# First stage: normalisation moved to the scalar engine, low parts to Pool, three sets of part buffers

## What is computed

```python
x = x + L0_xattn(_layernorm(x), ctx, ctx, Wq, Wk, Wv, Wo)      # softmax attention, 16 heads of 16
x = x + L0_ffn(_layernorm(x), ...)                              # ternary weights, 8-bit levels, width 1024
x = x + L1_xattn(_layernorm(x), ctx, ctx, ifgate_w, ...)        # gated linear attention, 8 heads of 32
x = x + L1_ffn(_layernorm(x), weight, gate_w, lora_U, lora_V)   # dense plus gated low-rank

def _layernorm(x, axis=-1, eps=1e-05):
    m = jnp.mean(x, axis=axis, keepdims=True)
    v = jnp.var(x, axis=axis, keepdims=True)
    return (x - m) / jnp.sqrt(v + eps)
```

## Time and profile before

| | |
|---|---|
| Median of three runs | 512.41 us (507.75, 512.41, 512.77) |
| The profiled execution | 512.96 us |
| Its span in the trace | 511.2 us |
| PE busy | 379.1 us (74%) |
| DVE busy | 322.7 us (63%) |
| ACT busy | 258.3 us (51%) |
| Pool busy | 188.3 us (37%) |
| Mean granted clock of TensorE | 0.868 of full speed |

### The profile page before, as it was taken

One profiled execution on the slowest core, in us unless ns is written; L12 is line 12 of the kernel. 1 busy time (PEld: TensorE's weight loads), 2 busy tenths in 40 slices (PEclk: granted clock), 3 DMA queues, 4 the chain that ended last, 5 costly groups with the idle time before them and its releaser, 6 DMA issues.

```text
span 511.2 us, 8639 instructions
## 1 busy us (share of the span) xinstructions
PE 379.1 (74%) x2897; PEld 260.6 (51%) x2897; DVE 322.7 (63%) x1040; ACT 258.3 (51%) x486; POOL 188.3 (37%) x220
## 2 busy tenths in 40 slices
PE   3986597898878893447776667663778999999955
PEld 3774354665656561123533434442666676776722
DVE  3885433366445575377889879743357877877752
ACT  2644233643534552567887987854243443543521
POOL 1119300000000001787898898850014334333330
PEclk9998867879999996565888998987599999999975
DMA  6699987645465400000000000000021221221100
GB/s 205 201 291 270 298 274 184 131 80 135 107 123 111 78 2 1 1 2 0 1 1 1 1 1 1 1 1 1 0 42 42 43 63 48 48 62 48 26 21 21
DMA packets 53675, 37.91 MB, mean 74 GB/s; under 512 B 21632, under 2 KB 49664, under 8 KB 53504
## 3 DMA queue, kind: packets, MB, share of 16 engines
q1 hardware_dynamic: 53120, 37.31, 29.3%
q10 hardware_dynamic: 512, 0.07, 0.2%
HBM read 28.90 MB, written 8.39 MB: 73 GB/s over the span
## 4 chain that ended last, share of the span: by engine, by line
PE 28%; DVE 19%; issue 19%; POOL 11%; DMA 11%; ACT 8%; SPq 3%; ACTq 0%; POOLq 0%; DVEq 0%
POOL rr L472 5%; DMA QT<-negmT 5%; PE PS L1108 4%; PE PS L1206 4%; DMA qst<-negmT 4%; DVE h L637 3%; PE PS L1097 3%; PE PS L1088 2%; DVE negm L577 2%; DMA scr_k<-kpart 2%; ACT pT L913 2%; SPq L311 2%; PE PS L1166 2%; POOL smd L464 2%; PE PS L1125 1%
## 5 line engine op out<-in xcount | busy, mean ns | idle before, releaser
L913 ACT ACTIVATE pT<-PS 128x512 f32<-128x512 f32 x64 | 36.5, 596 | 68.4 <-PE PS L1088 67.9
L577 DVE TENSOR_REDUCE negm<-PS 128x4 bf16<-128x512 f32 x64 | 42.5, 686 | 41.9 <-PE PS L1097 41.6
L447 POOL TENSOR_TENSOR sm<-sm,mhalf 128x1 f32<-128x1 f32 x16 | 9.2, 574 | 142.2 <-DVE sm L678 142.2
L435 POOL TENSOR_TENSOR kst<-kst,rows 128x1024 f32<-128x1024 f32 x16 | 38.3, 2393 | 3.3 <-ACT kst L983 3.3
L437 POOL TENSOR_TENSOR kst<-kst,rows 128x1024 f32<-128x1024 f32 x16 | 38.2, 2386 | 1.3
L472 POOL TENSOR_TENSOR rr<-ms,mhalf 128x8 f32<-128x8 f32 x16 | 26.4, 1649 | 31.1 <-DVE ms L860 31.1
L1280 PEld LDWEIGHTS PS<-QT,kBD 128*128 128x128 f32 x256 | 34.6, 196 | 0.9
L1280 PE MATMUL PS<-QT,kBD 128*128 128x128 f32 x256 | 34.6, 279 | 0.0
L1108 PE MATMUL PS<-pT,vx 128*32 128x128 f32 x512 | 29.9, 309 | 3.6 <-ACT pT L913 3.5
L628 DVE SCALAR_TENSOR_TENSOR pT<-PS,sm,rows 128x1024 f32<-128x1024 f32 x16 | 20.5, 1284 | 17.4 <-PE PS L1206 17.2
L1189 PE MATMUL PS<-w2q,h2T 128*128 128x256 bf16 x128 | 18.4, 292 | 17.5 <-ACT h2T L955 17.5
(11 more groups left out here) (222 smaller groups left out, 1045.4 us busy)
## 6 DMA issues: line engine op xcount, KB each, us to landing
scr_q<-qpart SPq DMA_DIRECT2D x8, 384.0 KB, 4.8
scr_k<-kpart SPq DMA_DIRECT2D x8, 384.0 KB, 5.5
rows<-in_rows SPq DMA_DIRECT2D x1, 2056.0 KB, 9.5
X<-in_x SPq DMA_DIRECT2D x8, 256.0 KB, 4.5
CTXT<-in_ctxT SPq DMA_DIRECT2D x8, 256.0 KB, 4.8
cTb<-in_ctxT SPq DMA_DIRECT2D x16, 128.0 KB, 3.4
kBD<-in_ctxT SPq DMA_DIRECT2D x64, 32.0 KB, 1.9
vx<-in_ctx SPq DMA_DIRECT2D x16, 128.0 KB, 2.6
```

Of the source, the lines that this page charges most:

```text
L435: gp.tensor_tensor(n2[p.slot], n2[p.slot], ln2g, ALU.mult).then_inc(b_g2, 1)
L577: v.tensor_reduce(negm[:, 4 * hg:4 * hg + 4], PS[:, 2 + hg % 2, :].rearrange("p (h k) -> p h k", h=4), AX_X, ALU.max, negate=True).then_in ...
L913: s.activation(pT[:, hg, :], PS[:, hg % 2, :], ACT.Exp, scale=float(DH0) ** -0.5).then_inc(a_e, 1)
```

## The change

ACT takes over the normalisation as `Identity` with a scale and a bias from memory (1/sigma and minus mean over sigma), at the start of its turn. DVE makes minus the mean (`nm`), Pool the product `mr` after its power. Pool takes over the two subtractions that make the low parts, ahead of its power in each turn, and has one turn stage more. A third set of `qpart` and `kpart` lies in `kBD`, which stage C uses later. Pool waits for all its low parts before it begins its list of constants.

```diff
...
+        mr = [sb(f"mr{i}", [128, GP]) for i in range(2)]; nm = [sb(f"nm{i}", [128, GP]) for i in range(2)]
...
-        qpart = [sb(f"qpart{i}", [128, PARTS, GP, KC * S], BF16) for i in range(2)]
-        kpart = [sb(f"kpart{i}", [128, PARTS, GP, KC * S], BF16) for i in range(2)]
+        kBD = [sb(f"kBD{i}", [128, 4, KC, S]) for i in range(2)]
+        third = [kBD[i][:].rearrange("p j c t -> p (j c t)").bitcast(BF16)[:, 0:PARTS * GP * KC * S]
+                 .rearrange("p (n j x) -> p n j x", n=PARTS, j=GP) for i in range(2)]
+        qpart = [sb(f"qpart{i}", [128, PARTS, GP, KC * S], BF16)[:] for i in range(2)] + [third[0]]
+        kpart = [sb(f"kpart{i}", [128, PARTS, GP, KC * S], BF16)[:] for i in range(2)] + [third[1]]
...
-        p_stored = [sem(f"p_parts_stored{i}") for i in range(2)]
+        p_stored = [sem(f"p_parts_stored{i}") for i in range(3)]; p_pw = sem("p_power_ready")
...
                 for buf, scr in ((qpart, scr_q), (kpart, scr_k)):
                     sp.dma_start(scr[g].rearrange("n j p x -> p (n j) x"),
-                                 buf[g % 2][:].rearrange("p n j x -> p (n j) x")).then_inc(p_stored[g % 2], 16)
+                                 buf[g % 3].rearrange("p n j x -> p (n j) x")).then_inc(p_stored[g % 3], 16)
...
-                if isinstance(at.b, int):
-                    g = at.b // GP
-                    sp.wait_ge(p_stored[g % 2], (g // 2 + 1) * STORED)
+                g = at.b // GP
+                sp.wait_ge(p_stored[g % 3], (g // 3 + 1) * STORED)
...
-            def turn_p(f, _ln, _b):
+            def turn_p(f, _ln, _b, c):
+                if c:
+                    for n, buf, ready in ((0, kpart, p_low), (1, qpart, p_parts)):
+                        flat = [buf[c.b % 3][:, i].rearrange("p j (c t) -> p j c t", c=KC) for i in range(PARTS)]
+                        pool.wait_ge(p_mid, c.b * 2 + n + 1)
+                        gp.tensor_tensor(flat[2], rest[n][:].rearrange("p (j c t) -> p j c t", j=GP, c=KC), flat[1],
+                                         ALU.subtract).then_inc(ready, 1)
                 if f:
                     pool.wait_ge(p_ve, f.b + 1)
                     done(pool, p_ln, f, -1)
-                    gp.tensor_tensor(rs[f.slot % 2][:], ve[f.slot % 2][:], mhalf[:, 0:GP], ALU.pow).then_inc(p_rs, 1)
-
-            pipeline(pool, NG, 4, 3, turn_p)
+                    gp.tensor_tensor(rs[f.slot % 2][:], ve[f.slot % 2][:], mhalf[:, 0:GP], ALU.pow).then_inc(p_pw, 1)
+                    pool.wait_ge(p_pw, f.b + 1)
+                    gp.tensor_tensor(mr[f.slot % 2][:], nm[f.slot % 2][:], rs[f.slot % 2][:], ALU.mult).then_inc(p_rs, 1)
+
+            pipeline(pool, NG, 4, 4, turn_p)
             pool.wait_ge(p_rs, NG)
+            pool.wait_ge(p_low, NG)
+            pool.wait_ge(p_parts, NG)
...
             for i in range(2):
                 step(gp.memset(vx2[i][:, :, DH1:64], 1.0))
+                pool.wait_ge(p_stored[2], STORED * (NG // 3))
                 step(gp.memset(kBD[i][:], 0.0))
...
-            def turn_p(f, a, b, c):
-                def parts(at, n):
...
-                def part_low(n):
-                    _product, flat, r4 = parts(c, n)
-                    dve.wait_ge(p_mid, c.b * 2 + n + 1)
-                    return v.tensor_tensor(flat[2], r4, flat[1], ALU.subtract)
...
                     dve.wait_ge(p_hi, b.b * 2 + n + 1)
-                    v.tensor_tensor(r4, product, flat[0], ALU.subtract).then_inc(p_rest, 1)
-
-                if a:
-                    dve.wait_ge(p_rs, a.b + 1)
-                    done(dve, p_tr, a, -1)
-                    for i in range(GP):
-                        last = v.tensor_scalar(lnb[a.slot % 2][:, i, :], X[:, a.b * GP + i, :], mv[a.slot % 2][:, i, 0:1],
-                                               rs[a.slot % 2][:, i:i + 1], ALU.subtract, ALU.mult)
-                    last.then_inc(p_ln, 1)
-                if c:
-                    part_low(0).then_inc(p_low, 1)
-                    part_low(1).then_inc(p_parts, 1)
+                    v.tensor_tensor(rest[n][:].rearrange("p (j c t) -> p j c t", j=GP, c=KC),
+                                    PS[:, bank + b.slot % 2, :].rearrange("p (c j t) -> p j c t", c=KC, j=GP),
+                                    buf[b.b % 3][:, 0].rearrange("p j (c t) -> p j c t", c=KC),
+                                    ALU.subtract).then_inc(p_rest, 1)
+
                 if f:
                     dve.wait_ge(p_x[f.slot], 32 * (f.used + 1))
                     c1.start(f)
@@ -521,11 +511,14 @@
                     f_bn = c1.mark(v.bn_stats(st[f.slot % 2][:, 6:12], X[:, f.b * GP + 1, :]))
...
+                    done(dve, p_ln, f, -1)
                     v.bn_aggr(mv[f.slot % 2][:, 0, :], st[f.slot % 2][:, 0:6])
...
                     done(dve, p_rs, f, -1)
+                    v.tensor_scalar(nm[f.slot % 2][:], mv[f.slot % 2][:, :, 0], -1.0, None, ALU.mult)
                     v.tensor_scalar(ve[f.slot % 2][:], mv[f.slot % 2][:, :, 1], EPS, None, ALU.add).then_inc(p_ve, 1)
                     c1.end()
...
-            pipeline(dve, NG, 4, 4, turn_p)
+            pipeline(dve, NG, 4, 3, turn_p)
...
-                    flat = [buf[b.slot % 2][:, i].rearrange("p j (c t) -> p j c t", c=KC) for i in range(2)]
+                    flat = [buf[b.b % 3][:, i].rearrange("p j (c t) -> p j c t", c=KC) for i in range(2)]
...
-                if b:
-
-                    if not (isinstance(b.b, int) and b.b < 2):
-                        act.wait_ge(p_stored[b.slot % 2], (b.used * 2 + b.slot // 2) * STORED)
+                if f:
+                    act.wait_ge(p_rs, f.b + 1)
+                    done(act, p_tr, f, -1)
+                    for i in range(GP):
+                        last = s.activation(lnb[f.slot % 2][:, i, :], X[:, f.b * GP + i, :], ACT.Identity,
+                                            scale=rs[f.slot % 2][:, i:i + 1], bias=mr[f.slot % 2][:, i:i + 1])
+                    last.then_inc(p_ln, 1)
+                if b:
+
+                    if b.b >= 3:
+                        act.wait_ge(p_stored[b.b % 3], b.b // 3 * STORED)
                     mid_k = high(0, p_k, 4, kpart)
...
```

More of the change, by code:

```diff
@@ L231, in build @@
         g_a = sem("g_a_parts_chain"); g_m = sem("g_max_parts_chain")
-        kBD = [sb(f"kBD{i}", [128, 4, KC, S]) for i in range(2)]
         vx2 = [sb(f"vx2{i}", [128, H1, 64]) for i in range(2)]
@@ L330, in turn_a @@
                 if f and not (isinstance(f.b, int) and f.b < 4):
-                    if not isinstance(f.b, int) and f.slot == 0:
-                        for i in range(2):
-                            sp.wait_ge(p_stored[i], NG // 2 * STORED)
                     load_stacks(f)
@@ L486, in _, with turn_p, part_rest @@
             c1 = Chain(dve, p_st, 2)
-            def turn_p(f, a, b, c):
-                def parts(at, n):
+            def turn_p(f, _a, b):
+                def part_rest(n):
                     bank, buf = ((4, kpart), (2, qpart))[n]
-                    return (PS[:, bank + at.slot % 2, :].rearrange("p (c j t) -> p j c t", c=KC, j=GP),
-                            [buf[at.slot % 2][:, i].rearrange("p j (c t) -> p j c t", c=KC) for i in range(PARTS)],
-                            rest[n][:].rearrange("p (j c t) -> p j c t", j=GP, c=KC))
-                def part_low(n):
-                    _product, flat, r4 = parts(c, n)
-                    dve.wait_ge(p_mid, c.b * 2 + n + 1)
-                    return v.tensor_tensor(flat[2], r4, flat[1], ALU.subtract)
-                def part_rest(n):
-                    product, flat, r4 = parts(b, n)
-                    dve.wait_ge(p_hi, b.b * 2 + n + 1)
-                    v.tensor_tensor(r4, product, flat[0], ALU.subtract).then_inc(p_rest, 1)
-                if a:
-                    dve.wait_ge(p_rs, a.b + 1)
-                    done(dve, p_tr, a, -1)
-                    for i in range(GP):
-                        last = v.tensor_scalar(lnb[a.slot % 2][:, i, :], X[:, a.b * GP + i, :], mv[a.slot % 2][:, i, 0:1],
-                                               rs[a.slot % 2][:, i:i + 1], ALU.subtract, ALU.mult)
-                    last.then_inc(p_ln, 1)
-                if c:
-                    part_low(0).then_inc(p_low, 1)
-                    part_low(1).then_inc(p_parts, 1)
+                    dve.wait_ge(p_hi, b.b * 2 + n + 1)
+                    v.tensor_tensor(rest[n][:].rearrange("p (j c t) -> p j c t", j=GP, c=KC),
+                                    PS[:, bank + b.slot % 2, :].rearrange("p (c j t) -> p j c t", c=KC, j=GP),
+                                    buf[b.b % 3][:, 0].rearrange("p j (c t) -> p j c t", c=KC),
+                                    ALU.subtract).then_inc(p_rest, 1)
                 if f:
```

## The result

| | before | changed |
|---|---|---|
| Median, runs of the first comparison | 511.53 us (4 runs, 507.75 to 512.77) | 520.66 us (4 runs, 516.82 to 521.80) |
| Median, a later comparison | 511.72 us (17 runs) | 519.89 us (6 runs) |
| Profiled execution, span | 512.96, 511.2 us | 520.18, 518.4 us |
| PE, DVE, ACT, Pool busy | 379.1, 322.7, 258.3, 188.3 us | 373.1, 311.1, 266.4, 207.6 us |

The ratio is 1.0195 (95% interval 1.0143 to 1.0247), and 1.0139 (1.0070 to 1.0208) in the later comparison: slower, though neither interval settles whether by more or by less than 2%. A ratio leaves out runs that lie more than 1.5% above the fastest of their kernel, so that one very fast run of the kernel before (501.90 us, in the comparison of e1 to e4) can move it: e1's ratio, 1.0166, stands well above that of its medians, 1.010.

The account below looks back on a forecast made before the run. It took a 4.51 us loop through DVE, PE and ACT in stage p, no single engine, as the bound. Late constants cost 11.7 us, 4.7 come back: +7.0 on 512.96 gives 520.0 us, range 515 to 526.

Parts of the forecast that it names:

- The loop: Stage p: normalisation on ACT behind the queries' middle part lengthens each group from 4.51 to 5.50 us.
- Pool's subtraction: Pool's turn in stage p: a 128 x 512 subtraction takes 1.29 us, hidden unless it takes over 2.2.
- The constants: Between stages p and A: Pool's 9.3 us list, behind the last low part, delays stage A to 63.9, +11.7 us.
- What comes back: Early stage A: drained transfer queues and PE's clock return 4.7 us: first row 3.2, clock 1, third row 0.5.
- a shift passes to the end: After the early turns of stage A everything follows PE's turns, so the remaining delay reaches the end.
- The third set: Stage p: a third set of parts removes all ACT's waits for stores, up to 12.7 us.
- pays back almost exactly: End of stage p for PE: longer loops and later start offset the removed store waits, 52.5 against 52.2.
- worth nothing: DVE in stage p: losing four instructions a group and gaining a tiny one brings no time.
- Rival D: Stage p gets slower as idle PE loses clock or Pool's subtraction exceeds 2.2: +12, 525 us, chance 0.12.
- A: Early stage A: drained queues and clock give back 8.1 us, so +3.6, 516.5 us; chance 0.15.
- B: Stage p: the loop stays at 4.51 us, constants are done by 58.9, so +2.0, 515 us; chance 0.04.
- C: Stage p: the loop opens to PE's own 4.1 us a group, so -5.5, 507.5 us; chance 0.03.

Follow-up runs that it names:

- e1: Changed kernel with the eleven constants issued in Pool's idle stretches of stage p instead of behind the last low part: 515.93 us against 510.83 before, ratio 1.0166.
- e4: Changed kernel with the normalisation back on DVE, low parts on Pool, third set and late constants kept: 527.17 us, ratio 1.0325 to the kernel before.
- e3: Kernel before with two added waits only, so Pool's constants come after the low parts of all groups: 520.21 us against 510.83, ratio 1.0178.
- e5: Changed kernel with ACT normalising a turn earlier, ahead of the queries' middle part, constants still late: 518.84 us against 511.72 before, ratio 1.0125.
- e6: Changed kernel with constants in Pool's idle stretches and normalisation ahead of the queries' middle part: 511.60 us against 511.72 before, ratio 1.0019.
- e7: Changed kernel run again, unedited, in a later comparison: 519.89 us, ratio 1.0139 to the kernel before.
- e8: Changed kernel with two sets of parts instead of three: 526.05 us against 519.89 for the changed kernel beside it, ratio 1.0267 to the kernel before.
- e2: Kernel before with the third set of parts alone, normalisation, low parts and constants unmoved: 509.17 us against 510.83, ratio 0.9953.

## Why the prediction was right

Forecast 520.0, range 515 to 526; measured 520.66. The closeness flatters. The forecast was +7.0 us on an execution of 512.96, which lies 1.4 above the median that the kernel before then had; by the medians the change costs 9.1 us (511.53 to 520.66) and 8.2 in the later comparison, between the two profiled executions 7.2. The order of size and the deciding step were right; a hit within a microsecond is luck. Step by step:

- **The loop**: 5.50 forecast, 5.51 measured, and by its parts: the pair 1.08 for 1.08, the middle part in the chain, hi-part to rest as before. Group 2 was normalised at 16.82 (16.6), group 7 at 44.38 (44.1), and the last rest was read at 52.8 (52.5).
- **Pool's subtraction**: 1.29 forecast, 1.16 measured. The straight line between fp32 rows was 0.13 too long for this form. The effect is 0.1 us.
- **The constants**, the step that decides: first one at 54.99 (54.5), count done at 64.26 (63.9), PE at 64.36, though the profile names no releaser where the prediction expected Pool's name. e3 shows it to be enough for the whole loss, e5 to e6 that removing it gives 7.2 us; from the changed kernel itself to e1 it gives 4.7.
- **What comes back**: 4.7 forecast, 4.5 measured (12.15 at the start, 7.64 at the end). Its terms were off in ways that cancel: turn 0 gave 2.75 for 3.2, since PE's own work up to 72 us hid the landed row; the clock gave 1.85 for 1.0; turn 2 lost 0.40 where I had 0.5 back. The weights did not go out at the same time as before: `w2f` was issued at 61.80, not 58.6, and took 9.2 us, to 71.0, and the row issued at 69.55 took 1.7 all the same. That "a shift passes to the end" after turn 2 was wrong too: it went down to 5.66 and back to 7.40. In the second execution, e7, 12.76 at the start is 5.94 at the end, 6.8 back; that the first gave 4.5 is in part luck.
- **The third set**: no store waits were left, as forecast. That it "pays back almost exactly" held for the end of stage p within 0.6 us. It is the one part for which a gain was measured, 6 us between e8 and the changed kernel and about 2 in e2.
- **DVE "worth nothing"** was right for the time. But I had costed its new `nm` at next to nothing, and it takes 1.11 us when it meets Pool's subtraction:

```profile
33.76 1.11 DVE L521 TENSOR_SCALAR nm<-mv 128x2 f32<-128x2 f32 x1
34.79 0.15 DVE L522 TENSOR_SCALAR ve<-mv 128x2 f32<-128x2 f32 x1
```

  What covers it is DVE's idle time before the rest of the queries (1.90 us). In e4 the instruction that is held back is on the loop, with no such cover.
- **Rival D** (the clock falls in stage p) did not come: with 1.40 us idle in 5.51, PE's projections stayed at 1.89. In e4, with 2.02, they did not in three groups of six.
- **Rivals A, B and C** needed the loop to stay short or about 8 us to come back; the loop did not, and the two executions gave 4.5 and 6.8. e5 is rival B made real, a short loop with the constants late. B priced it at +2.0 us, and it measured +7.1 by the medians, so B's price was far too low: the last low part ended at 51.6, not 49.5, with 1.8 us of ACT's waiting for a store before it, and the first row took 4.8 us, so that at the last shifted product 3.5 of the 8.9 us of later start had come back, not 4.7. C's loop of 4.1 us never came about.

Not forecast: that 5 us are left in e1, without the constants, and nothing in e6. With the constants in the idle stretches the longer loop costs 5.2 us by the medians; with the constants late, e5 against the changed kernel, the same step is worth 1.1. The parts therefore don't add up to the whole: late constants alone cost 9.4 (e3), the rest of the change alone 5.1 (e1), both together 8 to 9. The traces show how the longer loop hides behind late constants. e5 begins stage A 3.2 us before the changed kernel, but its first row goes out at 66.27, while `w2f` is in flight, and takes 4.8 us instead of 1.7: the first shifted product is only 0.7 us sooner, PE has waited 3.65 us for it, and the next one is 1.1 later. Waiting longer let the transfers drain. That is one execution of each; no run isolates it.

## What to carry to other kernels

When work moves onto an engine, read what stands behind it in that engine's list, down to the next count that others wait for: here a list of fills that had always been free became 9.3 us on the path, with two wait instructions. When a step moves off a busy engine, look for the loop rather than for the busy share: DVE looked full (4.70 of 5 us busy from 15 to 20 us), but the loop through DVE, PE and ACT set the pace, and moving its first link onto ACT, behind the middle part of the queries, made it longer. Two moves that each look harmless can need each other: low parts on Pool with the normalisation on DVE was the slowest kernel of all.

## What the runs showed of the hardware

- A `tensor_scalar` of two elements on DVE took 1.11 to 1.13 us instead of 0.17 beside a Pool subtraction, in five groups of the changed kernel; in e4 a pair of 128 x 256 took 2.34 instead of 0.74 beside two. `tensor_tensor` from PSUM and SBUF took 0.69 in every group, also where it overlapped Pool's power or the start of a subtraction.
- TensorE stayed at its upper level (2.4 GHz) in the changed kernel with idle stretches of 1.40 us in 5.5, granted clock 1.00 from 10 to 50 us. In e4, with 2.02 us idle before each group, it fell towards the lower one (1.2 GHz) in three groups of six.
- A 4 KB transfer took 1.6 to 1.8 us in the last turns of stage A and where the weights had nearly landed, and 4.4 to 7.9 while one of the 1 MB weight loads or the 2 MB load was in flight. After the waits of 3.5 to 4 us that these caused, PE ran at half the clock (0.50 from 64 to 69 us and from 84 to 89 us before, from 94 to 99 in the changed kernel), and those turns took 10.1 to 10.7 us instead of 8.
